# First stage of a graph network on one core: source and destination terms of a head in one product, operand tiles built by GpSimd, the mask in one fp32r product

## What is computed

```
h    = x @ W[a]                                  # 12 heads, 256 x 32 each
th   = tanh(h)
attn = (th @ w_src) + (th @ w_dst).T             # 256 x 256 of a head: one number per row node and one per column node
attn = where(attn >= 0, attn, 0.2 * attn)
attn = softmax(where(~adj, -999, attn))
out  = elu(attn @ h + b)
gate = sigmoid(x @ H_w.T + H_b)
y    = layernorm(x + gate * out + (1 - gate) * x)
```

## Time and profile before

| | |
|---|---|
| median of the runs | 3484.99 us (3483.56 to 3487.18) |
| the profiled execution | 3486.2 us |
| its span | 3484.4 us |
| mean granted clock of TensorE | 0.983 |
| busy time of TensorE, its weight loads | 3194.1 us (92%), 2674.6 us (77%) |
| busy time of VectorE, ScalarE, GpSimd | 2405.0 us (69%), 2091.2 us (60%), 1038.4 us (30%) |
| score products of stage 1 (lines 554 to 556) | from 39.7 us to 1061.6 us |

### The profile page before, as it was taken

The page is one execution under the profiler, slowest core; times in us unless marked ns, Lnnn a source line. Parts: engine busy times, 40 slices in busy tenths (PEclk is TensorE's granted clock), DMA queues, the critical chain, the costliest instruction groups (busy, mean ns, idle before and its releaser), DMA issues. The chain is left out here.

```text
span 3484.4 us, 81776 instructions
## 1 busy us (share of the span) xinstructions
PE 3194.1 (92%) x24736; PEld 2674.6 (77%) x24736; DVE 2405.0 (69%) x8345; ACT 2091.2 (60%) x6323; POOL 1038.4 (30%) x998
## 2 busy tenths in 40 slices
PE   7999899989995999999997999999997999999998
PEld 5777777777774887887886887887886888787886
DVE  4766666666674776776776776776776677676776
ACT  5777777777883555555554555555554555555554
POOL 1333333333332232323223123232332132323223
PEclk9999999999997999999999999999999999999999
DMA  2001001001001111111011011011111011111110
GB/s 69 26 26 31 27 26 31 31 22 31 31 20 63 31 36 36 37 35 41 31 41 65 26 41 41 31 41 32 41 36 40 26 36 36 41 31 41 33 38 29
DMA packets 107156, 124.32 MB, mean 36 GB/s; under 512 B 39680, under 2 KB 106176, under 8 KB 106176
## 3 DMA queue, kind: packets, MB, share of 16 engines
q1 hardware_dynamic: 106688, 118.57, 10.8%
HBM read 68.22 MB, written 50.33 MB: 34 GB/s over the span
## 5 line engine op out<-in xcount | busy, mean ns | idle before, releaser
L760 POOL TENSOR_TENSOR a_residual<-a_x,a_br 128x384 f32<-128x384 f32 x192 | 191.9, 1021 | 1583.1 <-DVE a_mix L896 1527.8
L827 ACT ACTIVATE a_probs<-a_logits,a_nmax 128x256 f32<-128x256 f32 x1152 | 574.3, 506 | 17.7 <-issue 14.9
L73 PE MATMUL a_pj<-a_xt_hi,a_w_lo 128*128 128x256 f32 x1728 | 516.7, 299 | 67.8 <-DVE a_xt_lo L861 67.8
L918 DVE CUSTOM_DVE_ANT_0 a_logits<-a_s,a_mask 128x256 f32<-128x256 f32 x1152 | 439.8, 418 | 162.2 <-PE a_s L1005 137.6
L807 ACT ACTIVATE a_qk_hi<-a_pj,a_bc 128x256 fp32r<-128x256 f32 x576 | 241.9, 471 | 449.4 <-PE a_pj L75 449.4
L74 PE MATMUL a_pj<-a_xt_lo,a_w_hi 128*128 128x256 f32 x1728 | 487.2, 282 | 0.0
L75 PE MATMUL a_pj<-a_xt_hi,a_w_hi 128*128 128x256 f32 x1728 | 486.9, 282 | 0.0
L443 DVE CUSTOM_DVE_ANT_0 g_v<-g_z,g_v 128x256 f32<-128x256 f32 x768 | 294.6, 420 | 270.7 <-ACT g_v L341 261.8
L73 PEld LDWEIGHTS a_pj<-a_xt_hi,a_w_lo 128*128 128x128 f32 x1728 | 327.9, 190 | 138.6 <-DVE a_xt_lo L861 91.5
L347 ACT ACTIVATE g_exps<-g_v,g_nmax 128x256 f32<-128x256 f32 x768 | 382.2, 505 | 0.8 <-DVE g_nmax L443 0.6
L875 DVE TENSOR_SCALAR a_probs<-a_probs,a_recs 128x256 f32<-128x256 f32 x1152 | 357.8, 353 | 20.6
(11 more groups left out here) (116 smaller groups left out, 8192.1 us busy)
## 6 DMA issues: line engine op xcount, KB each, us to landing
a_x<-y SPq DMA_DIRECT2D x96, 384.0 KB, 3.1
y<-a_out SPq DMA_DIRECT2D x96, 384.0 KB, 2.5
g_x<-x SPq DMA_DIRECT2D x32, 384.0 KB, 3.1
y<-g_out SPq DMA_DIRECT2D x32, 384.0 KB, 2.5
w_stage<-att_w SPq DMA_DIRECT2D x3, 2304.0 KB, 9.8
a_adj<-adj SPq DMA_DIRECT2D x96, 64.0 KB, 2.9
g_adj<-adj SPq DMA_DIRECT2D x32, 64.0 KB, 3.1
g_w_stage<-gat_w SPq DMA_DIRECT2D x1, 1152.0 KB, 5.7
```

What stands on the lines that cost most here:

```text
L73: pe.matmul(out, a[1], b[0], start=first, stop=False)
L827: last = act.activation(probs[:, i, t, :], logits[:, h % 2, t, :], ACT.Exp, scale=-1.0, bias=nmax[:, u, h, t:t + 1], accum_out=sums[:, u, ...
L918: last = dve.tensor_tensor_reduce(out=logits[:, j % 2, t, :], in0=s_ps[j % 2][:, t, :], in1=mask[u][:, t, :], scale=-HEAD_DIM ** -0.5, sca ...
```

## The change

The destination sums and the source sums are kept in two tiles of 128 rows each, half filled with ones: `z_left` (ones in the first 64 rows, source sums in the others) and `s_dst` (destination sums in the first 64 rows, ones in the others). GpSimd multiplies `s_dst` with the head selector into `z_right`, a tile for each head, four instructions of three heads each (`spread_targets`, at j = 10). A head's scores are then `z_left` times `z_right` for each 128 nodes, one product instead of two; and the mask of both halves is one product of 512 columns with the identity as the stationary operand, in fp32r. Per head that is three products instead of six. So that the spread can be done before the next sample begins, SD moves ahead of G in `PE_PLAN` (j = 9, G at j = 10), with the banks and waits that go with it: G now waits for the split of TT+1, LAST for the split of SD, X for G's tanh of the previous sample. SD's high part is two ScalarE instructions of 64 rows. VectorE builds fewer constants at the start; GpSimd waits for them.

```diff
--- before.py
+++ after.py
@@ -81,6 +81,7 @@
 
     STEPS = 9
+    HALF = P // 2
     QUAD = P // GAT_DIM
     GROUPS = GAT_HEADS // QUAD
@@ -93,7 +94,7 @@
         x_sb = [sb(f"x{p}", [P, NT, D]) for p in range(2)]
         adj_sb = [sb(f"adj{p}", [P, NT, N], U8) for p in range(2)]
-        mask = [sb(f"mask{p}", [P, NT, N], BF16) for p in range(2)]
+        mask = [sb(f"mask{p}", [P, NT, N], F32R) for p in range(2)]
         w_stage = sb("w_stage", [P, 2, DC, D])
         w_hi, w_lo = sb("w_hi", [P, 2, DC, D], F32R), sb("w_lo", [P, 2, DC, D], F32R)
@@ -104,15 +105,15 @@
         ones = sb("ones", [2 * 32, P], F32R)
         ident = sb("ident", [P, P])
-        ident_bf = sb("ident_bf", [P, P], BF16)
-        sel = sb("sel", [P, 2, GAT_HEADS])
-        sel_dst = sb("sel_dst", [P, GAT_HEADS, P], F32R)
-        sel_src = sb("sel_src", [P, GAT_HEADS, N], F32R)
+        ident_r = sb("ident_r", [P, P], F32R)
+        sel = sb("sel", [P, GAT_HEADS])
+        z_left = [sb(f"z_left{p}", [P, N], F32R) for p in range(2)]
+        z_right = [sb(f"z_right{p}", [P, GAT_HEADS, N], F32R) for p in range(2)]
         half_neg = sb("half_neg", [P, NT])
         xt_hi, xt_lo = sb("xt_hi", [P, DC, N], F32R), sb("xt_lo", [P, DC, N], F32R)
         th = sb("th", [P, NT, D])
         tt_hi, tt_lo = sb("tt_hi", [P, DC, N], F32R), sb("tt_lo", [P, DC, N], F32R)
-        sd = [sb(f"sd{p}", [P, N], F32R) for p in range(2)]
+        s_dst = [sb(f"s_dst{p}", [P, N], F32R) for p in range(2)]
 
 
@@ -145,6 +146,7 @@
         consts_ready, half_ready = sem("consts_ready"), sem("half_ready")
         w_hi_done, w_split, hb_ready = sem("w_hi_done"), sem("w_split"), sem("hb_ready")
+        z_right_done = sem("z_right_done")
         mask_ready, x_share, x_used = sem("mask_ready"), sem("x_share"), sem("x_used")
         pj_made = sem("pj_made")
@@ -163,18 +165,20 @@
 
 
-        X, H, TT, G, SD, LAST = 0, 2, 4, 6, 7, 8
+        X, H, TT, SD, G, LAST = 0, 2, 4, 6, 7, 8
+        Z_GROUP = 3
+        DST, SRC = slice(0, HALF), slice(HALF, P)
         ALL = tuple(range(DC))
 
 
         PE_PLAN = {0: [(X, ALL)], 1: [], 2: [(X + 1, ALL)], 3: [(H, (0, 1))], 4: [(H, (2,))], 5: [(H + 1, (0, 1))], 6: [(H + 1, (2,))],
-                   7: [(TT, ALL)], 8: [(TT + 1, ALL)], 9: [(G, ALL)], 10: [(SD, ALL)], 11: [(LAST, ALL)]}
+                   7: [(TT, ALL)], 8: [(TT + 1, ALL)], 9: [(SD, ALL)], 10: [(G, ALL)], 11: [(LAST, ALL)]}
 
         PLAN = {j: k for j, made in PE_PLAN.items() for k, chunks in made if DC - 1 in chunks}
...
 
 
-        BANK = {X: 0, X + 1: 1, H: 0, H + 1: 0, TT: 1, TT + 1: 0, G: 1, SD: 0, LAST: 1}
+        BANK = {X: 0, X + 1: 1, H: 0, H + 1: 0, TT: 1, TT + 1: 0, SD: 1, G: 0, LAST: 1}
         HI_STEPS = {H: 1, H + 1: 2, SD: 3}
         READ_STEPS = {X: 1, X + 1: 2, TT: 3, TT + 1: 4, SD: 5}
@@ -242,7 +246,7 @@
         @block.gpsimd
         def _(pool):
-            start(pool, mask_ready, x_share, x_used, ctx_bias, summed, rstd_done, var_eps, ln_done)
+            start(pool, z_right_done, mask_ready, x_share, x_used, ctx_bias, summed, rstd_done, var_eps, ln_done)
             pool.memset(half_neg[:, :], -0.5).then_inc(half_ready, 1)
 
@@ -251,6 +255,17 @@
 
                 pool.tensor_scalar(mask[u][:, :, :], adj_sb[u][:, :, :], -1.0, -MASKED_GAT, ALU.add, ALU.mult).then_inc(mask_ready, 1)
+
+            def spread_targets(half, u, prev):
+
+                if prev:
+                    pool.wait_ge(scores, at(GAT_HEADS, *prev, GAT_HEADS))
+                held(pool, pj_read, reads(half, u, SD), passed)
+                for h in range(0, GAT_HEADS, Z_GROUP):
+                    heads = slice(h, h + Z_GROUP)
+                    shape = [P, Z_GROUP, N]
+                    pool.tensor_tensor(z_right[u][:, heads, :], f32(s_dst[u][:, :]).unsqueeze(1).to_broadcast(shape),
+                                       sel[:, heads].unsqueeze(2).to_broadcast(shape), ALU.mult).then_inc(z_right_done, 1)
 
             def inverse_std(half, u, eps):
@@ -293,11 +308,15 @@
                     if prev and j == 9:
                         total(*prev)
+                    if nxt and j == 10:
+                        spread_targets(*nxt, prev)
                     if prev and j == 11:
                         inverse_std(*prev, 4 * EPS)
...
 
             pool.wait_ge(half_ready, 1)
+            pool.wait_ge(consts_loaded, 6 * 16)
+            pool.wait_ge(consts_ready, 1)
             every_slot(pool, 0, slot)
 
@@ -316,7 +335,8 @@
                 act.wait_ge(pj_made, step(half, u, k) + 1)
                 if k == SD:
-                    act.activation(sd[u][:, :], ps[:, 0:N], ACT.Identity).then_inc(pj_hi, 1)
+                    act.activation(z_left[u][SRC, :], ps[SRC, 0:N], ACT.Identity)
+                    act.activation(s_dst[u][DST, :], ps[DST, 0:N], ACT.Identity).then_inc(pj_hi, 1)
                     return
                 t = k - H
@@ -374,9 +394,11 @@
             start(dve, pj_read, hi_copied, back_read, maxed, inverted, pt_odd_read, ctx_min, elu_done, gated, bn, aggr)
             dve.wait_ge(consts_loaded, 6 * 16)
-            dve.tensor_copy(ident_bf[:, :], ident[:, :])
-            dve.tensor_copy(sel_dst[:, :, :], sel[:, 0, :].unsqueeze(2).to_broadcast([P, GAT_HEADS, P]))
-            dve.tensor_copy(sel_src[:, :, :], sel[:, 1, :].unsqueeze(2).to_broadcast([P, GAT_HEADS, N])).then_inc(consts_ready, 1)
+            dve.tensor_copy(ident_r[:, :], ident[:, :])
+            for p in range(2):
+                for part, rows in ((z_left, DST), (s_dst, SRC)):
+                    last = dve.tensor_scalar(part[p][rows, :], ident[rows, 0:1].to_broadcast([HALF, N]), 0.0, 1.0, ALU.mult, ALU.add)
+            last.then_inc(consts_ready, 1)
             for m in range(2):
                 dve.wait_ge(w_hi_done, m + 1)
@@ -397,9 +419,9 @@
                     return
                 dve.wait_ge(pj_hi, at(len(HI_STEPS), half, u, HI_STEPS[SD]))
-                for q in (1, 3):
+                for part, q in ((z_left, 3), (s_dst, 1)):
                     rows = slice(32 * q, 32 * q + 32)
-                    last = dve.tensor_tensor(sd[u][rows, :], ps[rows, 0:N], f32(sd[u][rows, :]), ALU.subtract)
+                    last = dve.tensor_tensor(part[u][rows, :], ps[rows, 0:N], f32(part[u][rows, :]), ALU.subtract)
                 last.then_inc(pj_read, 1)
 
@@ -474,18 +496,18 @@
 
                     if k == X:
-                        pe.wait_ge(pj_read, reads(half, u, SD) - len(READ_STEPS))
+                        pe.wait_ge(gate_done, at(NT, half, u, 1 - NT))
                     elif k == TT:
                         pe.wait_ge(back_read, at(NT, half, u, -NT))
                         pe.wait_ge(pj_hi, at(len(HI_STEPS), half, u, HI_STEPS[H + 1]))
-                    elif k in (X + 1, LAST):
-                        pe.wait_ge(gate_done, at(NT, half, u, 0 if k == X + 1 else 1))
+                    elif k == X + 1:
+                        pe.wait_ge(gate_done, at(NT, half, u, 0))
                     elif k in (H + 1, TT + 1):
                         pe.wait_ge(pj_hi, at(len(HI_STEPS), half, u, HI_STEPS[{H + 1: H, TT + 1: H + 1}[k]]))
...
                             pe.wait_ge(pj_read, reads(half, u, X + 1))
                     else:
-                        pe.wait_ge(pj_read, reads(half, u, {H: X, G: TT, SD: TT + 1}[k]))
+                        pe.wait_ge(pj_read, reads(half, u, {H: X, SD: TT + 1, G: TT + 1, LAST: SD}[k]))
                 if k in (X, X + 1):
                     t = k - X
@@ -545,15 +567,13 @@
                         half, u = cur
                         if j == 0:
-                            pe.wait_ge(pj_read, reads(half, u, SD))
                             pe.wait_ge(mask_ready, at(1, half, u, 1))
+                        if j % Z_GROUP == 0:
+                            pe.wait_ge(z_right_done, at(GAT_HEADS // Z_GROUP, half, u, j // Z_GROUP + 1))
                         pe.wait_ge(maxed, at(GAT_HEADS, half, u, j - 1))
+                        pe.matmul(z_ps[j % 2][:, :, :], ident_r[:, :], mask[u][:, :, :], start=True, stop=False)
                         for t in range(NT):
-                            z = z_ps[j % 2][:, t, :]
-
-                            pe.matmul(z, sel_dst[:, j, :], sd[u][:, :], start=True, stop=False)
-                            pe.matmul(z, sd[u][:, t * P:(t + 1) * P], sel_src[:, j, :], start=False, stop=False)
-                            last = pe.matmul(z, ident_bf[:, :], mask[u][:, t, :], start=False, stop=True)
+                            last = pe.matmul(z_ps[j % 2][:, t, :], z_left[u][:, t * P:(t + 1) * P], z_right[u][:, j, :], start=False, stop=t == NT - 1)
                         last.then_inc(scores, 1)
                     for k, chunks in PE_PLAN[j] if nxt else ():
@@ -1092,10 +1112,10 @@
         for q, name in enumerate(("L0_gnn_w_dst", "L0_gnn_w_dst", "L0_gnn_w_src", "L0_gnn_w_src")):
             w_sd[rows, 32 * q + h] = a[name][h, :, 0]
```

(5 more changed lines are left out.)

## The result

The changed kernel takes **3526.34 us** (median of 4 runs, 3525.0 to 3528.52); the kernel before, run beside it, 3486.09 us (4 runs, 3483.56 to 3489.42). The ratio is **1.0119, with a 95% interval from 1.0103 to 1.0134**: 40 us slower. The forecast was 3526.

The account below looks back on a forecast made before the run. The prediction followed one sample's chain through TensorE, ScalarE and VectorE, with TensorE no hard bound. From 3486 us it added 6 for longer samples and 34 for clock falls: 3526 us, range 3470 to 3550.

Parts of the forecast that it names:

- Score block, 0.25 us less: TensorE's score products of one head: one of 512 columns and two of 256 replace six, 0.47 us instead of 0.72.
- The ReLU of head 7 at 17.93: ScalarE's ReLU of head 7 comes 17.93 us into a sample instead of 18.83, 0.90 us earlier through shorter score blocks.
- 13.75 us from there to the transposes of head 9: Chain from the ReLU of head 7 to TensorE's transposes of head 9: 13.75 us instead of 12.65, 1.10 us lost.
- SD waits for the second TT split, 5.44 us after that ReLU: TensorE's slot 9: SD needs VectorE's second TT split, 5.44 us after head 7's ReLU, so TensorE stands some 2.9 us.
- A sample 0.20 us longer: Each first-stage sample: 1.10 us lost by moving SD against 0.90 won by shorter score blocks; 6 us over 31 samples.
- The clock falls in four of five gaps: TensorE's granted clock halves for 3.4 us after the gap before SD: 0.8 x 1.4 x 30 samples = 34 us.
- The sum, 6 + 34: Whole kernel: 3486 us plus 6 for longer samples plus 34 for clock falls gives 3526 us.
- The mask as one fp32r product: Mask product of 512 columns, estimated at 0.23 us, bounds 0.12 and 0.46; on GpSimd the wider mask stays one instruction.
- the clock holds: Rival: the gap before SD brings falls in few samples, so only the 6 us count: 3492 us; chance 0.17.
- The gain reaches the end: Rival: moving G costs nothing, so 0.90 us a sample is kept: 3458 us; chance 0.15.
- GpSimd late: Rival: GpSimd's broadcast products take 4.5 us, so z(0), head 0's score block, waits 0.5 us a sample: 3542 us; chance 0.08.

## Why the prediction was right

- **Score block, 0.25 us less.** Right for ScalarE, too much for TensorE's own next step. The ReLUs of heads 3, 4, 6 and 7 come 0.24, 0.49, 0.75 and 0.93 us earlier in the sample (241.24, 243.19, 249.04 and 251.74 from 233.84; before, 590.80, 593.00, 599.11 and 601.99 from 583.16), where 0.25, 0.50, 0.75 and 0.90 were forecast. But the block takes 0.55 to 0.57 us from its first product to the next step and not 0.47, only 0.17 less than before: the next product starts 0.32 us behind the wide one, not 0.23.
- **The ReLU of head 7 at 17.93.** 17.90.
- **13.75 us from there to the transposes of head 9.** 265.54 - 251.74 = 13.80 in the sample where the clock held. Partly luck: z(10) and z(11) took 0.55 and 0.57 us where 0.47 stood, and G and LAST 2.02 and 2.03 where 2.13 stood.
- **SD waits for the second TT split, 5.44 us after that ReLU.** 5.45; SD starts at 23.40. The gap is 2.67 us (2.7 in the profile forecast), in all 30 samples.
- **A sample 0.20 us longer.** 32.11 to 32.16 us where the clock held, against 32.1. The gain of 0.90 stands in the trace as the earlier ReLU of head 7 (0.93), the loss of 1.10 as 14.21 us from that ReLU to the next sample where 13.06 passed before (1.15); with G first they came out as 0.92 and 1.14.
- **The clock falls in four of five gaps.** 24 of 30, with a granted clock of 0.96 in the stage. A fall cost 1.6 us and not 1.4: 24 x 1.6 = 38 us where 34 stood, and the filled gap gives 39. That it rested on three gaps was its weakness: the kernel with the order alone, at 2.41 us, shows 11 of 30, and the same "four in five" missed there by 15 us. The fraction was lucky in its size: a run of falls and then a sample without one is the rhythm of this loop, which the prediction didn't work out, and not a chance for each gap. That falls would come was in the rows.
- **The sum, 6 + 34.** From the first to the last score product the stage grew by 45.9 us (30 x 0.23 for the samples, 38 for the falls, 1 not accounted for). The start is 2.2 us earlier and stage 2, which nothing touched, 4.5 us shorter in the profiled execution. The start was put at nothing with 3 us either way; kernels with the same start differ by more (35.5 to 39.7 us until the first score product). Stage 2 had no term. Its clock differs between executions: it held some 61 us at half clock before and 46 us after. Over all kernels here stage 2 is shortest (2360.8 us) where it held 38 us and longest (2372.4 us) where it held 69 us. So 3526 hits partly by luck: the dearer falls and the shorter start and stage 2 cancel.
- **ScalarE.** Its long wait for the gate went, as forecast. Each SD copy on 64 partitions takes 0.38 us.
- **GpSimd.** A product takes 1.47 us where 1.83 was taken, inside the bounds of 1.0 and 3.7, and is hidden even when made twice.
- **The mask as one fp32r product.** Missed, and no term of the sum: beyond its columns I gave the wider mask no price but GpSimd's. Against two bf16 products it costs 0.17 us a sample, by the argument above its weight load of 199 ns; the bf16 mask takes 13 us off the kernel after.

Of the rivals, *the clock holds* gives the right time when it is made to hold: 3487 us with the gap filled, 3492 forecast. *The gain reaches the end* was barred by VectorE's block, as argued; with G first, where the move costs nothing, it gives 3457, and 3458 was worked out. *GpSimd late* falls: no score product waits for it in the order of the change.

## What to carry to other kernels

Before moving a step to an earlier slot, measure when its last operand is ready after the event that fixes the slot, and how long the engine stands if the step put behind it is no longer there to fill the hole. A hole of 2 to 3 us on TensorE in each turn of a loop can cost more than its length: here the clock fell at four of five holes of 2.67 us, 1.6 us each time. If the hole can't be closed, half of it filled with idle products was enough here. After a move, follow the next wait through all engines: a copy put first lost 17 us until the instruction that waited for the delayed gate product was moved as well. And compare stage by stage: the untouched stage 2 differed by up to 12 us between executions, as much as many of the effects looked for here.

## What the runs showed of the hardware

- How often a fall of the clock came with the gap ahead of SD: never in a steady sample at 0.43 and 1.50 us, 11 of 30 at 2.41, 24 of 30 at 2.67. In another place (z(0) waiting for GpSimd), 19 of 28 at 2.08 us. So the length alone doesn't decide. What TensorE did before differs between the two places, and so does the rhythm of samples and falls; neither was varied by itself, and this stays open.
- The Trainium skill (page "TensorE: Matmul & The Clock Gate", section "Why this matters for your kernels") warns of gaps over about 3 us. Here every gap was shorter, and the clock fell at 24 of 30: the measurement decides.
- Each of these falls was to the level of 1.2 GHz for 3.4 us. It cost 1.6 us in the kernel after, nearly all of the half that can be lost, and 1.3 to 1.5 us where it began before the gap was over.
- Six idle products of 384 columns in a gap of 2.67 us, which left 1.50 us of it open, did away with all falls in steady samples.
- The product behind an fp32r product of 512 columns started 0.32 us after it, at full clock.
- The weight load of an fp32r operand of 128 by 128 took 199 ns, of a bf16 one 99 ns, of the fp32 one at the transposes 145 ns.
- GpSimd's product of two broadcast inputs, 128 by 768, took 1.47 us, less than its sum of two full tiles of the same size, 1.83 us.
- An Identity copy out of PSUM on ScalarE takes 0.38 us for 64 partitions by 256 elements, as the one on 128 partitions did in the kernel before: the two halves take as long as two whole ones.
